# A conv-attention kernel whose cosine similarity takes its left operand and its exchanged halves from tokens before their norms, with the norms multiplied in as the tiles are copied

## The reference

```python
xf = x.reshape(B, C, N).transpose(0, 2, 1)
nrm = jnp.linalg.norm(xf, axis=-1, keepdims=True)
xn = xf / jnp.maximum(nrm, 1e-12)
sim = jnp.einsum('bnc,bmc->bnm', xn, xn)
val, idx = jax.lax.top_k(sim, K)              # K = 9
v = val / (val.sum(axis=-1, keepdims=True) + 1e-06)
def gcn_apply(feat, w, b):
    xt = feat @ w
    neigh = jax.vmap(lambda t, i: t[i])(xt, idx)
    return jnp.einsum('bnkc,bnk->bnc', neigh, v) + b
out = gcn_apply(xn, w1, b1)
out = jax.nn.silu(group_norm(out.transpose(0, 2, 1).reshape(B, C, H, W), gamma1, beta1))
...
```

## Time and profile before

| | |
|---|---|
| median of 3 runs | 685.54 us (684.87 to 685.59) |
| the profiled execution's own time | 687.54 us |
| its span, first to last instruction | 685.7 us |
| PE busy | 621.9 us (91%) |
| DVE, ACT, POOL busy | 536.6, 449.2, 499.2 us |
| mean granted TensorE clock | 0.98 of full |

### The profile page before, as it was taken

One profiled execution on the slowest core, in us unless ns is written; L12 is line 12 of the kernel. 1 busy time (PEld: TensorE's weight loads), 2 busy tenths in 40 slices (PEclk: granted clock), 3 DMA queues, 4 the chain that ended last, 5 costly groups with the idle time before them and its releaser, 6 DMA issues.

```text
span 685.7 us, 12336 instructions
## 1 busy us (share of the span) xinstructions
PE 621.9 (91%) x3824; PEld 310.4 (45%) x3824; DVE 536.6 (78%) x1008; ACT 449.2 (66%) x942; POOL 499.2 (73%) x534
## 2 busy tenths in 40 slices
PE   8878899898999999898999999999999999899874
PEld 6654535353444535353544435353535444333441
DVE  3357879788898889797888988898898988857821
ACT  2356477685868767784868768786868686743321
POOL 0224877788797978879797978788897979786810
PEclk9999999999999999999999999999999999979997
DMA  3002533434353535444363634445353534353411
GB/s 94 1 17 46 115 72 79 88 83 96 81 110 69 109 77 110 80 90 92 80 109 62 113 79 108 87 87 100 91 94 63 109 77 98 74 108 78 63 32 31
DMA packets 148722, 55.76 MB, mean 81 GB/s; under 512 B 138008, under 2 KB 138512, under 8 KB 148656
## 3 DMA queue, kind: packets, MB, share of 16 engines
q1 hardware_dynamic: 148656, 54.97, 39.6%
HBM read 12.87 MB, written 4.32 MB: 25 GB/s over the span
## 4 chain that ended last, share of the span: by engine, by line
PE 33%; POOL 24%; issue 16%; DVE 10%; DMA 9%; ACT 7%; SPq 1%; POOLq 0%; ACTq 0%; DVEq 0%
PE pC L974 18%; POOL adj L389 10%; PE pS L930 5%; POOL adj L384 5%; DMA rbc<-rn_row 4%; DMA rn_row<-rnT 4%; ACT adj L527 2%; PE pB L775 2%; DVE kstat L607 2%; ACT ek L458 2%; POOL res L407 2%; PE pA L814 2%; POOL qn L348 2%; POOL xn L372 2%; DVE top L683 2%
## 5 line engine op out<-in xcount | busy, mean ns | idle before, releaser
L974 PE MATMUL pC<-adj,xt 128*64 128x512 f32 x992 | 233.1, 603 | 2.9 <-POOL adj L395 1.6
L389 POOL TENSOR_TENSOR adj<-maskT,adj 128x128 f32<-128x128 f16 (+3 forms) x127 | 163.5, 1287 | 27.0 <-DMA maskT<-mask 25.2
L683 DVE MAX8 top<-pS 128x8 f32<-128x1024 f32 x128 | 155.6, 1224 | 33.1 <-ACT adj L527 32.9
L701 DVE MATCH_REPLACE8 mask<-top,pS 128x1024 uint16<-128x1024 f32 x128 | 155.2, 1213 | 0.0
L930 PE MATMUL pS<-xn 64*128 64x512 f32 x256 | 146.9, 661 | 7.3 <-issue 6.5
L930 PE MATMUL pS<-xn,xsw 64*128 64x512 f32 x256 | 146.2, 662 | 2.9 <-DVE mask L701 2.9
L527 ACT COPY adj<-pS 128x1024 f32<-128x1024 f32 x128 | 128.3, 1003 | 30.3 <-PE pS L932 30.2
L384 POOL TENSOR_TENSOR adj<-maskT,adj 128x128 f32<-128x128 f16 (+6 forms) x111 | 128.4, 1157 | 0.0
L974 PEld LDWEIGHTS pC<-adj,xt 128*64 128x64 f32 x992 | 64.0, 137 | 103.3 <-issue 94.7
L395 POOL TENSOR_TENSOR adj<-adj,selves 128x128 f32<-128x128 f32 x127 | 58.5, 461 | 8.7
L932 PEld LDWEIGHTS pS<-mark,place 64*128 64x128 f16 x256 | 24.7, 97 | 77.3 <-issue 77.3
(11 more groups left out here) (154 smaller groups left out, 1097.0 us busy)
## 6 DMA issues: line engine op xcount, KB each, us to landing
xs<-x SPq DMA_DIRECT2D x32, 128.0 KB, 2.8
vbc<-v_row SPq DMA_DIRECT2D x32, 128.0 KB, 2.9
rbc<-rn_row SPq DMA_DIRECT2D x30, 128.0 KB, 2.9
xsw<-xn SPq DMA_DIRECT2D x30, 128.0 KB, 2.3
out<-res SPq DMA_DIRECT2D x30, 128.0 KB, 2.3
maskT<-mask SPq DMA_TRANSPOSE x128, 3.1
cst<-packed SPq DMA_DIRECT2D x1, 471.5 KB, 3.6
y1sw<-y SPq DMA_DIRECT2D x2, 128.0 KB, 2.3
```

Source lines behind the costliest of these rows:

```text
L389: pool.tensor_tensor(above, m[:, r, 0:r + 1, :].bitcast(F16), above, ALU.mult).then_inc(done["upper"], 1)
L683: dve.max(top[b % 2][:, r, 0:TOP], pS[r % 2][:, :]).then_inc(done["tile_top"], 1)
L701: dve.match_replace(out=mask[n % MASKS][:, :], in_to_replace=top[b % 2][:, r, 0:TOP], in_values=pS[r % 2][:, :], imm_value=ONE_BITS).then_ ...
L974: mm = pe.matmul(ps[h * C:(h + 1) * C, 0:H], xt[:, t % NJ, t // NJ, :], adj[b % 2][:, t, h * H:(h + 1) * H], start=(t == 0), stop=(t == NT ...
```

## The change

The similarity's left side becomes `y1`, and the exchange copies halves of `y1`, not of `xn`. A row of the tile is then too large by the norm of its token, so ACT's copy of the tile multiplies row by row with `rn`. DVE searches and marks in the unscaled tile, which has the same order within a row; its eight values are multiplied with `rn` once a sample, in a new DVE instruction ahead of their sum. `y1` and `rn` get two buffers each. POOL's `rn` gets two more waits (for the copies and the row sums two samples back), ACT's `y1` waits for the tiles two samples back in place of the `xn` before, and the exchange moves from the end to the head of SP's `unit` stage. For sample 0 the eight matmuls into `pC`, the DVE product into `xsw` and the buffer `y1sw` go. The constants `XSCALE` and `MARK` change their values.

```diff
-        "unit": [122.814, 124.0739, 139.8554],
+        "unit": [111.8545, 122.814, 124.0739],
...
             def unit(b):
+                yield
+                sp.wait_ge(*of("y1_ready", b))
+                sp.wait_ge(*of("sim_ps", b - 2, NT))
+                for h in range(2):
+                    sp.dma_start(xsw[b % 2][(1 - h) * C:(2 - h) * C, :], y1[b % 2][h * C:(h + 1) * C, :]).then_inc(done[f"swapped{b % 2}"], 16)
...
-                yield
-                sp.wait_ge(*of("xn_ready", b))
-                sp.wait_ge(*of("sim_ps", b - 2, NT))
-                for h in range(2):
-                    sp.dma_start(xsw[b % 2][(1 - h) * C:(2 - h) * C, :], xn[b % 2][h * C:(h + 1) * C, :]).then_inc(done[f"swapped{b % 2}"], 16)
...
                 pool.wait_ge(*of("ss_read", b, 2))
-                pool.tensor_tensor(rn[:, :], ssq[:, :], minus_half[:, :], ALU.pow).then_inc(done["rn_ready"], 1)
+                pool.wait_ge(*of("sim_copied", b - 2, NT))
+                pool.wait_ge(*of("v_tot", b - 2))
+                pool.tensor_tensor(rn[b % 2][:, :], ssq[:, :], minus_half[:, :], ALU.pow).then_inc(done["rn_ready"], 1)
...
-                act.wait_ge(*of("xn_ready", b - 1))
-                act.activation(y1[:, :], x1[b % XBUFS][:, :], ACT.Identity, bias=st["mi"][:, 15:16],
+                act.wait_ge(*of("sim_ps", b - 2, NT))
+                act.activation(y1[b % 2][:, :], x1[b % XBUFS][:, :], ACT.Identity, bias=st["mi"][:, 15:16],
...
                     act.wait_ge(*of_tile("sim_ps", n))
+                    act.wait_ge(*of("rn_ready", b))
                     if b >= 2:
                         act.wait_ge(*of_tile("tile_used", n - 2 * NT))
-                    act.copy(adj[b % 2][:, r, :], pS[r % 2][:, :]).then_inc(done["sim_copied"], 1)
+                    act.activation(adj[b % 2][:, r, :], pS[r % 2][:, :], ACT.Copy, scale=rn[b % 2][:, r:r + 1]).then_inc(done["sim_copied"], 1)
...
                 dve.wait_ge(*of("tile_top", b, NT))
+
+                dve.wait_ge(*of("tile_mask", b, NT))
+                dve.wait_ge(*of("rn_ready", b))
+                best = top[b % 2][:, :, 0:TOP]
+                dve.tensor_tensor(best, best, rn[b % 2][:, :].unsqueeze(2).broadcast_to([P, NT, TOP]), ALU.mult).then_inc(done["top_scaled"], 1)
...
-                    src = xn if r // NJ == h else xsw
+                    src = y1 if r // NJ == h else xsw
```

More of the change, by code:

```diff
@@ L17 @@
 TOP = 8
-XSCALE = 0.25
+XSCALE = 2.0 ** -12
 SSCALE = XSCALE * XSCALE
-MARK = -2.5 * SSCALE
+MARK = -2.5 / 16
 EPS = 1e-5
@@ L157, in build @@
         x1 = [sb(f"x1_{i}", [P, H]) for i in range(XBUFS)]
-        y1 = sb("y1", [P, H])
+        y1 = [sb(f"y1_{i}", [P, H]) for i in range(2)]
         sq = sb("sq", [P, H])
         xn = [sb(f"xn{i}", [P, H]) for i in range(2)]
-        y1sw = sb("y1sw", [P, H])
         xsw = [sb(f"xsw{i}", [P, H]) for i in range(2)]
         ssq = sb("ssq", [P, NT])
-        rn = sb("rn", [P, NT])
+        rn = [sb(f"rn{i}", [P, NT]) for i in range(2)]
         rnT = sb("rnT", [NT, P])
@@ L207, in build @@
             mi_stat mi_aggr mi_spread mi_mean_ps mi_minus mi_dev mi_veps mi_rstd mi_bias y1_ready
-            sq_ready ss_ps ss_read rn_ready rows exchanged first_swapped rn_T rnT_copied rn_saved rn_back xn_ready swapped0 swapped1
+            sq_ready ss_ps ss_read rn_ready rows rn_T rnT_copied rn_saved rn_back xn_ready swapped0 swapped1
             xt1_ps xt1_copied sim_ps sim_copied self_ready tile_top tile_mask turned0 turned1 turned2 diagonal upper lower late_lower late_upper late_diagonal late_y late_res
-            v_tot v_rec v_T vT_copied v_saved v_back
+            top_scaled v_tot v_rec v_T vT_copied v_saved v_back
             g1_ps g1_read g1_stat g1_aggr g1_shift g1_spread g1_mean_ps g1_minus g1_dev g1_veps g1_rstd g1_scale g1_bias
@@ L369, in unit @@
                 pool.wait_ge(*of("sim_ps", b - 2, NT))
-                if b > 2:
-                    pool.wait_ge(*swapped(b - 2))
-                pool.tensor_tensor(xn[b % 2][:, :], y1[:, :], rbc[:, :], ALU.mult).then_inc(done["xn_ready"], 1)
+                pool.tensor_tensor(xn[b % 2][:, :], y1[b % 2][:, :], rbc[:, :], ALU.mult).then_inc(done["xn_ready"], 1)
             def weights(b):
@@ L506, in unit @@
                 act.wait_ge(*of("y1_ready", b))
-                act.activation(sq[:, :], y1[:, :], ACT.Square).then_inc(done["sq_ready"], 1)
+                act.activation(sq[:, :], y1[b % 2][:, :], ACT.Square).then_inc(done["sq_ready"], 1)
             def itself(b):
@@ L667, in unit @@
                     dve.wait_ge(done["rows"], 1)
[L668 to L671, removed]
+                    dve.tensor_tensor(xn[0][:, :], pB[:, :], y1[0][:, :], ALU.mult).then_inc(done["xn_ready"], 1)
                 else:
@@ L685, in tops @@
                 dve.wait_ge(*of("tile_top", b, NT))
+                dve.wait_ge(*of("tile_mask", b, NT))
+                dve.wait_ge(*of("rn_ready", b))
+                best = top[b % 2][:, :, 0:TOP]
+                dve.tensor_tensor(best, best, rn[b % 2][:, :].unsqueeze(2).broadcast_to([P, NT, TOP]), ALU.mult).then_inc(done["top_scaled"], 1)
+                dve.wait_ge(*of("top_scaled", b))
                 dve.wait_ge(*of("ss_read", b, 2))
@@ L907, in unit @@
                 if b == 0:
[L909 to L915, removed]
+                    for j in range(NJ):
+                        for h in range(2):
+                            t = h * NJ + j
+                            mm = pe.matmul(pB[h * C:(h + 1) * C, j * P:(j + 1) * P], rn[0][:, t:t + 1].broadcast_to([P, C]), ident,
+                                           start=True, stop=True)
+                    mm.then_inc(done["rows"], 1)
                 else:
-                    pe.transpose(pB[0:NT, P:2 * P], rn[:, :], ident).then_inc(done["rn_T"], 1)
+                    pe.transpose(pB[0:NT, P:2 * P], rn[b % 2][:, :], ident).then_inc(done["rn_T"], 1)
             def similarity(b, r):
@@ L922, in similarity @@
                     pe.wait_ge(*of("xn_ready", b))
-                    pe.wait_ge(*swapped(b))
+                    pe.wait_ge(*of_buffer("swapped", b, 2, 32))
                 warm(f"sim{r}", b)
```

4 lines of the change are left out of this document (removed).

## The result

The changed kernel takes **832.06 us** in the median of four executions (830.6 to 836.98), against 685.57 us for the kernel before, run beside it. The ratio is 1.2135, 95% interval 1.2066 to 1.2203: 146 us slower.

The account below looks back on a forecast made before the run. PE, busy 35.70 of 38.24 us, was taken as nearly full within a loop of waits; 14 x (8.8 + 1.3 + 0.1) + 4.5 - 1.0 = 146.3 on 687.54 gave 833.8, less 2.0 for the median: 832 us, range 806 to 858.

Parts of the forecast that it names:

- What it moves: SP's list: exchange waits for `y1`, holding tile 2, `v_row`, `vbc`; `g` 8.9 us later, `kstat` 8.8 us, 14 times.
- the 0.1 of the copy: ACT's scaled tile copy: 0.1 us longer each, one of eight on the loop, so +0.1 us, 14 times.
- Who waits: DVE's `g` waits some 8 us for `vbc` and holds `kstat` behind it; the loop shifts 8.8 us.
- the rival of the late masks alone: If `g` did not hold `kstat`, only POOL's delay of 5.3 us would count: about 765 us, chance 6%.
- The clock: PE stands still over 8 us, restarts at 1.2 GHz: 1.3 us more on the loop before `rn`'s transpose, 14 times.
- The rival without the clock: The clock recovers before L917 or PE's slack takes it: 814 us, chance 12%.
- The rival with more of it: PE stays slow for about 6 us and loses 3 us a period: 856 us, chance 12%.
- What it adds: ACT's scaled copy, +0.1 us 14 times; new DVE instruction 0; new waits of `rn` and `y1` cost nothing.
- The new instruction: DVE, once a sample behind the last mask: at most 0.68 us, covered by slack, so 0; uncovered under 9.5 us.
- What it removes: The exchange behind `xn` was hidden but for 0.28 us, counted as nothing; sample 0's matmuls save 1.0 us once.
- The work dropped at sample 0: Eight matmuls into `pC`, 0.87 us on the chain, with about 0.1 of DVE behind: -1.0 us, once.
- sample 1's delay: At sample 1 no `v_row` stands behind the exchange, only tiles wait: +4.5 us, once.

Follow-up runs that it names:

- e6: The kernel before with only SP's wait for `y1` added at the exchange's new place, the exchange of `xn` staying where it was: 808.61 us, ratio 1.1756.
- e3: The changed kernel with the exchange later in SP's list, behind tile 2's transpose, `v_row` and `vbc`, ahead of two transposes: 727.49 us, ratio 1.0587.
- e8: The changed kernel with 78 unread matmuls keeping PE busy ahead of the sums of squares in samples 2 to 14: 824.87 us, ratio 1.1998.
- e1: The changed kernel with the exchange of `y1` back at its old place in SP's list: 694.32 us, ratio 1.0077.
- e2: The changed kernel with the exchange of `y1` between `rn_row` and `rbc` in SP's list: 700.1 us, ratio 1.0168.
- e4: The changed kernel with 65 unread matmuls on PE ahead of the sums of squares in samples 2 to 14: 838.05 us, ratio 1.219.

## Why the prediction was right

The forecast was 832 us and the median is 832.06. That closeness is partly luck: two terms were off, and they cancel. And the sum was made for the profiled execution: it gave 833.8 there, where 831.58 was measured. The 2.0 us taken off for the median belonged to one execution of the kernel before; the changed kernel's median lies 0.5 above its profiled execution.

- **What it moves: right, in place and in size.** The sum from `y1` to `g` was 8.02 us and measures 8.05 in the period shown. Its parts: exchange and gap 1.21 as forecast; `v_row` to `vbc` 308.24 - 306.69 = 1.55, not 1.91; `vbc` to `g` 312.13 - 308.24 = 3.89, not 3.55. Over all fourteen periods the mean is 8.21. The bare wait of e6 shows the mechanism without the rest. The table gives 35.50 - 26.09 = 9.4 us for the stretch from `xn` to `kstat`, where 8.9 had been forecast with the 0.1 of the copy: 0.5 us a period too little.
- **Who waits: right.** e3, in which `vbc` is not behind the wait, loses 40 us instead of 146. So the rival of the late masks alone (765 us for the change as it is) describes a real but smaller part. e3 leaves two of its transposes late and costs 40 us, where its own expectation was 27; the clock falls there too, but how much of the 13 us is the clock's stays open.
- **The clock: right in its place, too large in its net size.** 1.3 us a period were forecast between `kstat` and `rnT`, and 1.35 are there, of which 1.1 go when e8 keeps PE busy. The prediction took all of it to stay on the loop. But 0.75 us comes back between `rnT` and `xn`, because a later `rn_row` no longer lands behind the load of `x`, a wait that the prediction did not look at; e8 gives 0.7 us net. Here the term was 18 us and is 9. The rival without the clock (814 us, a ratio of 1.187) is contradicted by the clock of 0.50 and 0.59 in the changed kernel up to L911, and its size by e8, whose interval begins at 1.197. The rival with more of it (856, a ratio of 1.249) lies beyond the interval of the result.
- **What it adds: the copy not contradicted, the DVE instruction too small.** The copy's 0.1 x 14 = 1.4 us measure as 1.3, with an interval from nothing to 2.8. The new instruction was priced at 0 as covered by slack, with 9.5 us as the bound, and costs 2.3 to 3.0 us where it stands alone. The bound for one duration, 0.68 us, was wrong as well: up to 1.7 us.
- **What it removes.** The exchange's being hidden before is borne out: e1 copies `y1` at the old place, e2 earlier still, and neither gains; beside the 0.5 to 0.6% of the added instructions, a gain of up to 0.2% could hide in e1's interval. The work dropped at sample 0 shows between the `kstat` of samples 1 and 2: 31.36 us before, 31.38 in e6, 30.59 in the changed kernel and 30.60 in e1, so 0.8 us where 1.0 was forecast.

By the table, a period grew by 1.35 - 0.75 + 9.41 = 10.0 us, where 8.8 + 1.3 + 0.1 = 10.2 were forecast. The twelve periods of the table, from sample 3 to 15, make 120.1 us. The stretch ahead of them, which holds sample 1's delay and the first full one, grew by 15.5 us (68.17 to 104.60 before, 68.01 to 119.89 now), where 4.5 + 10.2 were forecast. What lies behind the last `kstat` grew by 8.7 (10.2 forecast), and what lies ahead of the `kstat` at 68.17 is 0.2 shorter (1.0 forecast; the 0.8 saved at sample 0 meet a start that was 0.6 later). Together that is 144.1 us, the whole growth of the span from 685.7 to 829.8; the sum of the prediction was 146.3.

## What to carry to other kernels

In a queue that issues in order, a transfer is not early because its data is older: ask where in time the queue stands when it comes to it, and which transfers behind it are already due. Here the data was there 13 us earlier than before (`y1` against `xn`) and the transfer itself had been hidden, so nothing could be gained; what stood behind it was within 1 us of being needed. When a filling or a cover is tried as an experiment, look in its trace for the gap that is left: e4 and e8 differ by 13 matmuls and would have led to opposite answers.

## What the runs showed of the hardware that was not expected

- A small DVE product in SBUF (128x64) took 198 to 1,675 ns by what POOL was doing, and ended 0.08 us after POOL's instruction; a reduction of the same shape took 220 to 223 ns at the same place.
- A 4 KB write to DRAM held up the transfer that waits for it for 1.20 to 1.26 us from issue to issue where SP had issued the load of `x` (two transfers of 128 KB) at least 2.65 us before it, or had none left; where the load was at most 1.65 us ahead, for 1.66 to 3.49 us (before, changed, e1, e3, e6 and e8).
- In e4 a gap of 1.66 us on PE, behind eight microseconds of uninterrupted matmuls, was followed by a granted clock that went from 1.00 over 0.76 to 0.50, 1.2 GHz.
